# A multi-engine transformer kernel: preparing the vectors ahead of DVE's loop, and writing the first column of `past` on POOL instead of ACT

## The reference

```
h = layernorm(x, ln1_w, ln1_b);  hh = time_shift(h)          # column t is h[t-1], column 0 is zero
k, v, r = (h*m + hh*(1-m)) @ W    for m in (tmk, tmv, tmr)
x = x + (sigmoid(r) * wkv(time_decay, time_first, k, v)) @ Wo
h = layernorm(x, ln2_w, ln2_b);  hh = time_shift(h)
xk = h*cmk + hh*(1-cmk);  xr = h*cmr + hh*(1-cmr)
x = x + sigmoid(xr @ Wcr) * (square(relu(xk @ Wck)) @ Wcv)
```

## Time and profile before

| | |
|---|---|
| median of 3 runs | 1327.79 us (1325.93 to 1328.26) |
| the profiled execution | 1328.26 us |
| its span in the trace | 1326.9 us |
| granted PE clock, mean | 0.992 |
| busy: PE, DVE, ACT, POOL | 95%, 92%, 91%, 88% |
| instructions in the span | 23258 |

### The profile page before, as it was taken

The page is one execution under the profiler, slowest core; times in us unless marked ns, Lnnn a source line. Parts: engine busy times, 40 slices in busy tenths (PEclk is TensorE's granted clock), DMA queues, the critical chain, the costliest instruction groups (busy, mean ns, idle before and its releaser), DMA issues.

```text
span 1326.9 us, 23258 instructions
## 1 busy us (share of the span) xinstructions
PE 1259.4 (95%) x7177; PEld 920.5 (69%) x7177; DVE 1219.9 (92%) x2169; ACT 1204.1 (91%) x2291; POOL 1167.9 (88%) x1391
## 2 busy tenths in 40 slices
PE   2689999999999999999999999989999998999997
PEld 1346667777777777777777777766777876778777
DVE  7998999999999999999999999689998587988994
ACT  3789999999999999999999999967888899999874
POOL 6998999999999999999999998999988365756883
PEclk9899999999999999999999999989999999999998
DMA  6020000000000000000000000101000000000011
GB/s 184 1 78 1 1 17 1 1 1 1 1 1 1 2 1 1 1 1 2 1 1 1 1 1 25 33 26 32 1 1 1 1 1 1 1 17 17 25 32 41
DMA packets 26924, 18.54 MB, mean 14 GB/s; under 512 B 1072, under 2 KB 26160, under 8 KB 26800
## 3 DMA queue, kind: packets, MB, share of 16 engines
q1 hardware_dynamic: 26800, 17.05, 4.3%
HBM read 12.85 MB, written 4.19 MB: 13 GB/s over the span
## 4 chain that ended last, share of the span: by engine, by line
PE 31%; DVE 28%; issue 15%; POOL 13%; ACT 10%; DMA 1%; DVEq 1%; SPq 0%; ACTq 0%; POOLq 0%
PE ps L1257 5%; DVE ln_st L231 4%; PE ps L1236 4%; PE ps L1229 4%; DVE ab L383 4%; DVE now L366 4%; PE ps L1198 3%; ACT now L857 2%; PE ps L1307 2%; PE ps L1180 2%; PE ps L1245 2%; PE ps L1289 2%; DVE xc L423 2%; DVE xv L340 2%; DVE sr L333 2%
## 5 line engine op out<-in xcount | busy, mean ns | idle before, releaser
L1198 PEld LDWEIGHTS ps<-W,kf 128*128 128x128 f32 x2048 | 243.7, 192 | 31.0 <-issue 30.0
L1198 PE MATMUL ps<-W,kf 128*128 128x128 f32 x2048 | 248.8, 275 | 0.0
L1180 PE MATMUL ps<-xk,W 128*128 128x512 f32 x512 | 240.8, 593 | 0.0
L653 POOL TENSOR_SCALAR z<-X,ln_rs 128x128 f32<-128x128 f32 x384 | 170.3, 455 | 0.5 <-POOL ln_rs L647 0.4
L1180 PEld LDWEIGHTS ps<-xk,W 128*128 128x128 f32 x512 | 92.0, 191 | 89.4 <-issue 88.1
L899 ACT ACTIVATE kf<-ps 128x512 f32<-128x512 f32 x256 | 149.4, 585 | 2.8 <-PE ps L1180 2.7
L686 POOL TENSOR_TENSOR now<-now,ab 128x1024 f32<-128x1024 f32 x64 | 139.6, 2181 | 4.6 <-DVE ab L383 4.3
L906 ACT ACTIVATE kf<-kf 128x1024 f32<-128x1024 f32 x128 | 134.5, 1051 | 0.0
L737 POOL TENSOR_TENSOR W<-W,hsc 128x704 f32<-128x704 f32 x64 | 88.7, 1386 | 46.1 <-DVE W L505 45.8
L1077 PEld LDWEIGHTS ps<-idn,z 128*128 128x128 f32 x664 | 81.2, 143 | 66.4 <-issue 43.4
L1077 PE MATMUL ps<-idn,z 128*128 128x128 f32 x664 | 101.7, 276 | 17.3 <-POOL z L653 15.1
(11 more groups left out here) (182 smaller groups left out, 3720.6 us busy)
## 6 DMA issues: line engine op xcount, KB each, us to landing
X<-x_in SPq DMA_DIRECT2D x16, 256.0 KB, 4.8
xi<-x_in SPq DMA_DIRECT2D x16, 256.0 KB, 2.9
out<-X SPq DMA_DIRECT2D x16, 256.0 KB, 2.3
W<-weights SPq DMA_DIRECT2D x4, 832.0 KB, 6.8
W<-fp4w SPq DMA_DIRECT2D x1, 560.0 KB, 8.0
row<-rows SPq DMA_DIRECT2D x1, 192.0 KB, 3.0
wqkv<-qkv SPq DMA_DIRECT2D x1, 96.0 KB, 5.5
idn<-ident SPq DMA_DIRECT2D x1, 64.0 KB, 3.3
```

The source lines that it names most:

```text
L653: last = e.tensor_scalar(chunk(dst, j), chunk(src, j), rs[:, 0, j:j + 1], rs[:, 1, j:j + 1], ALU.mult, ALU.add)
L1180: e.matmul((pF0, pF1)[f % 2][:, :], w_of(r, WCK + f), xk[r % 2][:, :], start=True, stop=True).then_inc(kf_mm[f], 1)
L1198: last = e.matmul(chunk(pKV, j), kf[r % 3][:, f, j * 128:(j + 1) * 128], w_of(r, WCV + f), start=f == 0 and j == 0, stop=f == 3, skip_grou ...
```

## The change

`prepare_vectors` loses its tick condition and is called once ahead of DVE's loop. `first_past` moves from ACT's loop, where it stood behind `keep_past` with lag 8, to POOL's loop with lag 9, between `weights_divided` (which issues something in one tick only) and `norm1_rest`; its instruction is a tensor_scalar (times 1, plus 0) instead of an activation. Its waits are the same.

```diff
-            def prepare_vectors(u):
-                if u == 0:
-                    w.wait_ge(small_here, 48)
-                    e.tensor_scalar(omt[:, :, :], vec[:, TMK:TMR + 1, :], -1.0, 1.0, ALU.mult, ALU.add).then_inc(vecs_done, 1)
...
+            def prepare_vectors():
+                w.wait_ge(small_here, 48)
+                e.tensor_scalar(omt[:, :, :], vec[:, TMK:TMR + 1, :], -1.0, 1.0, ALU.mult, ALU.add).then_inc(vecs_done, 1)
...
+            prepare_vectors()
             for t in range(FIRST, TICKS):
                 bn1(t - 1)
...
                 init_stats(t + 1)
-                prepare_vectors(t + 1)
                 mix_k(t - 8)
...
+            def first_past(r):
+                if 0 <= r < NR and r % NB < 2:
+                    w.wait_ge(vecs_done, VECS)
+                    w.wait_ge(xm_done, 2 * r - 2)
+                    e.tensor_scalar(past[r % 2][:, :, 0:1], cp[:, :, r // NB:r // NB + 1], 1.0, 0.0, ALU.mult, ALU.add).then_inc(pads, 1)
...
                 weights_divided(t - 5)
+                first_past(t - 9)
                 norm1_rest(t - 4)
...
-            def first_past(r):
-                if 0 <= r < NR and r % NB < 2:
-                    w.wait_ge(vecs_done, VECS)
-                    w.wait_ge(xm_done, 2 * r - 2)
-                    e.activation(past[r % 2][:, :, 0:1], cp[:, :, r // NB:r // NB + 1], ACT.Identity).then_inc(pads, 1)
...
                 keep_past(t - 8)
-                first_past(t - 8)
```

More of the change, by code:

```diff
@@ L233, in stats @@
                 last.then_inc(g.stats, 1)
-            def prepare_vectors(u):
-                if u == 0:
-                    w.wait_ge(small_here, 48)
-                    e.tensor_scalar(omt[:, :, :], vec[:, TMK:TMR + 1, :], -1.0, 1.0, ALU.mult, ALU.add).then_inc(vecs_done, 1)
[L239 to L245, removed]
+            def prepare_vectors():
+                w.wait_ge(small_here, 48)
+                e.tensor_scalar(omt[:, :, :], vec[:, TMK:TMR + 1, :], -1.0, 1.0, ALU.mult, ALU.add).then_inc(vecs_done, 1)
+                e.tensor_scalar(capt[:, :], vec[:, TF, :], -1.0, CAP, ALU.mult, ALU.add).then_inc(vecs_done, 1)
+                e.tensor_tensor(cw[:, :, :], vec[:, CMK:CMR + 1, :], vec[:, LN2W:LN2W + 1, :].to_broadcast([128, 2, L]), ALU.mult).then_inc(vecs_done, 1)
+                e.tensor_tensor(cp[:, :, :], vec[:, CMK:CMR + 1, :], vec[:, LN2B:LN2B + 1, :].to_broadcast([128, 2, L]), ALU.mult).then_inc(vecs_done, 1)
+                w.wait_ge(vecs_done, 3)
+                e.tensor_tensor(cz[:, :, :], vec[:, LN2W:LN2W + 1, :].to_broadcast([128, 2, L]), cw[:, :, :], ALU.subtract).then_inc(vecs_done, 1)
+                w.wait_ge(ew_done, 1)
+                e.tensor_scalar(wneg[:, :], ew[:, :], -1.0, None, ALU.mult).then_inc(vecs_done, 1)
             def prepare(u):
```

## The result

The changed kernel takes 1342.72 us (median of 4 runs, 1340.33 to 1348.81), the kernel before 1327.61 (4 runs, 1325.93 to 1328.26). The ratio is 1.0122 (95% interval 1.0088 to 1.0158): 1.2% slower, where 1330.5 us and at most 1332.4 were forecast. The sign was right; the size, +15 us measured against +2.7 forecast, was more than five times too small. The profiled execution took 1343.09 us with a span of 1341.8, 14.9 more than before.

A forecast was written before the change was run, and what follows sets the result against it. DVE, gapless from 200 to 600 us, was taken as the bound, POOL having under 1% of room. 0.4 - 0.1 + 0.1 + 2.3 = +2.7; 1328.26 + 2.7 - 0.47 = 1330.5 us; 8-in-10 range 1327.6 to 1332.4.

The forecast's parts named there:

- Vectors ahead of the loop, +0.4: At the start, X2's statistics on DVE come 0.41 us later, most of the shift hidden by their load wait: +0.4 us.
- first_past off ACT, -0.1: Eight instructions leave ACT; only the second, at 87.77 us in the chain, stands in the way: -0.1 us.
- units 0 and 1, +0.1: On POOL at 64.84 us, part of unit 0's added 0.20 us disappears in an existing hold, unit 1 costs 0: +0.1 us.
- The instruction's own size, 0.20: first_past on POOL takes 0.20 us, like the small L611, with bounds 0.10 and 0.51; its wait costs nothing.
- One push, 0.39: In a layer round, POOL's late power is held by reader L333; beyond a 0.27 us reserve, 0.39 us reaches DVE's L319.
- DVE is 0.39 late and the phase between the two is as before, so the next first_past does it again: Units 16, 17, 32, 33, 48 and 49: each push costs DVE the same, 6 x 0.39 = +2.3 us.
- Absorbed: Rival in the layer rounds: the power isn't held, the 0.20 us only shortens L647's hold; 1328.2 us, chance 0.22.
- Held through all three readers: Rival in the layer rounds: the power waits out three DVE readers, 1.72 us late six times; 1338.5 us, chance 0.05.
- The clock: Rival: at the start or end, moved work escapes stretches of reduced clock; faster, about 1325 us, chance 0.05.
- The Trainium skill's rule: With holds of the page's full length, each of the six pushes costs 0.14 us more, and the sum is 1331.4 us.

The follow-up runs named there:

- experiment 1: Changed kernel with first_past back on ACT, so only the vector instructions moved: 1328.61 us, 1.0004 of the kernel before.
- experiment 2: Kernel before with only first_past moved to POOL, vector instructions left where they were: 1344.4 us, 1.0127 of the kernel before.
- experiments 7: Kernel before, first_past left on ACT, plus four one-column memory writes on POOL at first_past's new place and ticks: 1330.23 us, ratio 1.0022.
- experiment 9: Changed kernel with first_past at the end of POOL's tick, behind norm2_rest: 1330.85 us, 1.0023 of the kernel before.
- experiment 3: Changed kernel with first_past on POOL between the power and the multiplication behind it: 1329.8 us, 1.0015 of the kernel before.
- 8: Changed kernel plus four tiny DVE operations ahead of the first reader in units 16, 17, 32, 33, 48 and 49: 1333.24 us, ratio 1.0038.
- 4: Changed kernel with only each layer's first unit's first_past on POOL, the second unit's on ACT: 1339.19 us, 1.0078 of the kernel before.
- 11: Changed kernel plus one tiny DVE operation ahead of the first reader in units 17, 18, 33, 34, 49 and 50: 1345.87 us, ratio 1.0129.
- 12: Changed kernel with one first_past per layer on POOL, plus one tiny DVE operation in units 17, 33 and 49: 1334.36 us, ratio 1.005.
- experiment 10: Changed kernel with DVE's bn1 statistics between the first and second reader from unit 16 on: 1356.04 us, 1.0212 of the kernel before.

## Why the prediction was wrong in its size

- *Vectors ahead of the loop, +0.4.* Right in kind. The statistics of X2 start at 12.91 with a wait of 0.36 (the load landed later in that execution than before), 12.56 in experiment 1. Alone, the edit measures +0.04% with an interval that holds zero; in its trace the mixing is 0.4 to 0.5 us late in units 5 to 15, and 0.72 with both edits.
- *first_past off ACT, -0.1, and units 0 and 1, +0.1.* Too small to tell apart. Unit 0 is +0.59 late, unit 1 +0.99, and by unit 5 it is +0.72, start included: together they are 0.3 us above the terms. One trace can't settle this: with `first_past` alone on POOL (experiment 2) the mixing is 1.5 us late by unit 5, of which 1.2 come in the round that ends at unit 1, and with two memory writes 0.4 us early.
- *The instruction's own size, 0.20.* It takes 0.19 but stands 0.09 us behind L678 (an instruction there before followed without a gap), so POOL is 0.26 later. In the next round L678 itself starts 0.10 us behind L707's end, where it had followed without a gap. In the last three layers this appears behind every `first_past` and behind none of the memory writes; in most rounds of the first layer it appears in every kernel, the one before included. I have no cause for it. The forecast had neither gap, and both have a part in where L678 meets DVE's scalings.
- *One push, 0.39.* Right in kind, a little small: 0.47 in each of the first late rounds of three layers, 0.40 with four memory writes (in four rounds of six). L644's length (2.08), L646's (0.20) and, within 0.03, the scaling's (0.60) came as written.
- **The step that failed: "DVE is 0.39 late and the phase between the two is as before, so the next first_past does it again".** Of the six pushes only the three first ones cost 0.47; behind each of them the phase was not as before, and a layer loses 4.2 to 6.8 us instead of 0.8. I had taken the hold of L319 as a coupling that carries POOL's delay over to DVE whole. It does so while `arg_r` starts 0.12 us or more ahead of the first scaling (0.12 to 0.15 in experiments 7 and 9, neither of which has slow rounds). At 0.00 to 0.04, behind the gap of 0.10 us, the first scaling slips in (0.15 to 0.19 us long) in all fifteen rounds of five traces. In eight of them the second ends 0.03 behind `arg_r`, and what follows on DVE is 0.07 us nearer to POOL; in seven, at 0.00 to 0.02, neither is held and DVE is nearer by all of the 0.4. Why one and not the other stays open. The reserve of order between the power and its reader was 0.06 us.
- *Rivals.* "Absorbed" fell with L644's 2.08 us. "Held through all three readers" had the right mechanism and 0.05 of chance; I had priced it as 6 x 1.72 and thought it unlikely for the power in the first round, rightly. It struck the instruction before the power (z, 2.44 us instead of 0.45) one round later. It is the one rival that I should have followed into the second round. The clock had no part: it is 1.00 in 200 to 400 us, as before.
- *The Trainium skill's rule* (page "SBUF — State Buffer", section "SBUF: two separate sides": VectorE and GpSimd hold a shared port pair exclusively for a whole instruction) again fits in kind and not in length. L644 at 276.76 is held to about 277.20, 0.13 ahead of L332's end, and L339 and L325 run unstretched beside it at 0.74. Beside the z instructions readers do stretch (0.94 at 744.20). By the page's rule the forecast would have been 1331.4; neither length foresees the cascade.

What shows the cause, then: experiment 2 (all of it is `first_past`), 3, 8 and 9 (the same instruction without the cascade, by place or by phase), 7 (the push without the gaps and without the cascade), 4, 11 and 12 (how the phase is lost). Open is where the gap ahead of `arg_r` comes from, and what the 0.2 us would cost without it.

## What to carry to other kernels

Where two engines run without a gap at the same period, an instruction's price is not its length: lay their timelines side by side, write down the order margins (here 0.06 us between a power and a reader, 0.5 between `arg_r` and a scaling) and ask of every edit which margins change sign. Follow the push for at least two rounds, since the first can be right and the second another case. The holds showed as instructions that got longer and hardly as waits: between 200 and 600 us DVE lost 8.6 us, and its waits in the changed kernel add up to 2.9. So compare durations by line before looking at idle time. Look for the place of small work by its order too: the same eight instructions cost 1.9 us behind the power (experiment 3) and 2.9 at the end of the tick (experiment 9), against 15.

## What the runs showed that I had not expected

*When a waiting POOL instruction is let in.* The power (128x8, two SBUF inputs) is seen 624 times between 200 and 800 us in thirteen traces (all but experiment 10's). By its start against the first of the three readers, which follow without a gap:

| start | seen | extra time |
|---|---|---|
| 0.01 us ahead or more | 524 | none |
| less than that, to 0.02 behind | 13 | none to 0.04, but twice 1.92 |
| 0.03 behind or more | 87 | 0.43 to 0.57 for 77; once 1.90 (at 0.04); none for nine (at 2.2 or more, behind all readers) |

Extra time of 0.43 to 0.57 means let in shortly before the end of the reader that is running when the power comes (24 times the first: the power, 1.65 us long alone, then ends 1.50 to 1.52 us behind that reader), 1.9 shortly before the end of the third. So arriving 0.05 us later can be *cheaper* than arriving just at the reader's start. The z instructions that meet the readers scatter more. Of the twelve that start 0.12 to 0.14 ahead of the first reader, four take 1.98 or 1.99 us extra, two 0.57 and six none; those from 0.05 ahead to 0.3 behind are all held, by 0.44 to 1.66. Why one instruction is passed over once and another three times, no run here explains.

*A tiny DVE operation waits for the end of a POOL instruction.* The scalings (128x8) take 0.16 to 0.18 us alone. The first of them to start a tenth of a microsecond or more into `arg_r` ends mostly 0.02 or 0.03 us (at most 0.07) behind `arg_r`'s end, and takes up to 0.62 for it (L319 at 287.46 against L678 until 288.03; L318 of experiment 9 at 286.91 against 287.49); with the four memory writes behind `arg_r` it takes 0.71 and ends 0.03 behind theirs.

*Small POOL instructions.* Memory writes of one column follow each other by 0.03 us (four in 0.19 to 0.20 us); a 128x2 operation (`first_past`) takes 0.19, and in the changed kernel starts 0.08 or 0.09 behind the instruction ahead of it. It has a semaphore wait of its own, satisfied long before; that this is the reason is not shown.
